# Dealing the first layer's expert groups anew over its two score loops

## The chip, the cores and the metric

The kernel runs on one core of one Trainium2 chip. The metric is the device time of one execution in microseconds, lower is better. Before the change three runs took 1210.66 to 1214.54 us, median 1212.18 us. One further execution was taken with the hardware profiler: 1208.67 us, with a span of 1206.9 us from its first to its last instruction.

## The reference

Two transformer layers on x of shape 4 x 512 x 128. Only the first layer touches the change:

```python
xn = layernorm(x)
x = x + attention0(xn) + experts0(xn)

# attention0: 16 heads, bd = 16, windows of 64 positions
strain = disp_win - disp                       # for every offset j = 0..63
bond_logits = gelu(strain @ W_strain + rel_emb @ W_pos) @ W_bond
damage      = sigmoid(gelu(strain @ W_dmg + b_dmg) @ W_dmg_out + b_dmg_out)
logits      = bond_logits - 10 * damage        # then masked softmax over the window

# experts0: 16 experts, each token goes to 4 of them
h = t @ w1.T + b1 ; s = swiglu(h) ; y = s @ w2.T + b2   # summed with the gates
```

## The kernel before, in words

The first layer is one setup block, then for each half g = 0, 1 of the heads a **score loop** and a softmax block; the second layer follows. `first_layer` builds all of it, and each block is a set of five programs, one per engine, that run side by side and meet at the block's end.

**The score loop.** A score loop has 64 items (offsets j), eight to an iteration `it` = 0..7. VectorE forms the shifted difference of an item (L757) into one of four slots of the tile `ring`, ScalarE takes the gelu (L895, or L900, L901 and L903), TensorE reduces it over the width of a head (`reduce`, L957) into the PSUM tile LG. The slot is free again when TensorE has reduced it. In five items of eight TensorE forms one of the two differences itself from the tile DS (`strain`, L981 and L985), in PSUM tile SD, instead of VectorE. DS holds three bf16 parts of the input in partitions 0 to 95 and ones in partitions 96 to 98, which add a bias. ScalarE splits the input into the parts (L935, L937), VectorE forms the remainders (L863, L870), SyncE copies them over (L669) and counts them on `d_parts`. GpSimd clears DS's margins (L730, L731) and writes the ones (L732). After each four items ScalarE takes a tanh (L911) and VectorE adds the logits (L777).

**The experts.** Tokens are sorted by expert through DRAM: in the first loop GpSimd scatters rows with 64 indirect DMAs (L741). SyncE waits for all of them before it loads the first sorted rows. 20 **groups** of four tiles of 128 tokens are then worked off between the items. A group n takes these steps:

- SyncE loads its rows (`tokens`, L649, tile xl), its first weights (`weights1`, L656, tile w1s, two groups deep) and its second weights (`weights2`, L663, tile w2s, one group deep)
- TensorE turns the rows (`turn`, L1019) and VectorE moves them to SBUF (`move_in`, L813)
- TensorE computes the hidden layer (`hidden`, L1027), VectorE and ScalarE apply the gate function (`glu_in` L821, `sig` L917, `glu_out` L828)
- TensorE computes the output (`expert_out`, L1036), VectorE moves it out (`move_out`, L835), GpSimd computes where it goes (`goals`, L712 to L718) and scatters it with four indirect DMAs (`store`, L723).

**What sets the order.** Every engine's order is written out by hand. `MOE_ITS` and `moe_groups` (L61, L103) say which iteration works on which groups: the first loop's iterations 5, 6 and 7 on groups 0 to 5, the second loop's iterations 0 to 6 on groups 6 to 19, two groups A and B to an iteration. In `body(it)` TensorE turns the next iteration's A behind `reduce(7, it)`, B behind `strain(5, it, 0)`; A's output comes after `strain(7, it, 0)`, B's output in the next iteration. SyncE's order in the second loop is: the 12 DS copies, eight first weights, four second weights, and only then the rows of the first two groups. A loop's block ends when SyncE has seen the last stores land (`d_ys`), GpSimd is done, and the other engines are through; in the second loop SyncE also starts `fetch(0)` and `fetch(1)` (L592) in it, which read the outputs back.

Of the kernel before, what the change touches and what calls it, by code (L numbers as in the profile page):

```python
# [21 lines left out]
B, T, C = 4, 512, 128  # L22
# [7 lines left out]
TP = PAD + T + 1  # L30
# [29 lines left out]
ZQ = 12  # L60
MOE_ITS = ((5, 6, 7), (0, 1, 2, 3, 4, 5, 6))  # L61
XROW = C + 2 * K0
# [40 lines left out]
def moe_groups(g, it):  # L103

    if it not in MOE_ITS[g]:
        return None, None
    first = 2 * (len(MOE_ITS[0]) * g + MOE_ITS[g].index(it))
    return first, first + 1

# [78 lines left out]
def first_layer(nc, t_in, l0, sb, psum, sem, ident, ACC, nhalf, stats, mv, rstd, carried):  # L188
# [34 lines left out]
    lones = sb("lones", [P, 4, 32], F32, l0)  # L223
# [20 lines left out]
    with ExitStack() as su:  # L244
# [332 lines left out]
    tok_turned, tok_moved, h_ready, xg_ready, sig_ready, s_ready, y_ready, y_used = (  # L577
        sem(n) for n in ("moe_turned", "moe_moved", "h_ready", "xg_ready", "sig_ready", "s_ready", "y_ready", "y_used"))
    d_scatter, d_w2, goals_ready = sem("d_scatter0"), sem("d_w2_"), sem("goals_ready")
    d_xl, d_ys, d_w1 = ([sem(f"{what}_{n}_") for n in range(2)] for what in ("d_xl", "d_ys", "d_w1"))  # L580
# [33 lines left out]
    for g in range(G):  # L614
        with ExitStack() as lp:
# [3 lines left out]
            xsT, t2 = attT[:, G - 1, 0, :], attT[:, G - 1, 1, :]  # L619
# [20 lines left out]
            PYf = PY[:].rearrange("p n c -> p (n c)")  # L640
            groups = [n for it in MOE_ITS[g] for n in moe_groups(g, it)]

            @block.sync
            def _(sp):
# [19 lines left out]

                sp.wait_ge(small_pool, 5 + 2 * g)
                for n, ready, count in ((0, parts_act, 1), (1, parts_act, 2), (2, parts_dve, 2)):
# [3 lines left out]
                if g == 0:  # L670
# [9 lines left out]
                    sp.wait_ge(small_dve, 8)  # L680
                first, end = groups[0], groups[-1] + 1
                weights1(first)
                weights1(first + 1)
                weights2(first)
                if g == 0:
                    sp.wait_ge(d_scatter, 16 * TT * K0)
                tokens(first)
                tokens(first + 1)
                for n in range(first, end, 2):
                    if n > first:  # L690
                        weights2(n)
                    if n + 2 < end:
                        weights1(n + 2)
                        tokens(n + 2)
                        weights1(n + 3)
                    weights2(n + 1)
                    if n + 2 < end:
                        tokens(n + 3)
                for n in range(2):
                    sp.wait_ge(d_ys[n], 64 * (end // 2))  # L700
                if g == G - 1:
# [4 lines left out]
            def _(pool):  # L706
# [24 lines left out]
                pool.memset(DS[0:96, :, :, PAD + T:TP], 0.0).then_inc(small_pool, 1)  # L731
                pool.memset(DS[96:99], 1.0).then_inc(small_pool, 1)  # L732
                pool.wait_ge(small_pool, 6 + 2 * g)
                for q in range(JQ - 1 if g else ZQ):
# [16 lines left out]
            def _(v):  # L751
# [85 lines left out]
                def body(it):  # L837
                    A, B_ = moe_groups(g, it)
                    before = moe_groups(g, it - 1)[1]
                    move_in(A)  # L840
# [28 lines left out]
                v.wait_ge(parts_act, 2 * g + 2)  # L869
                v.tensor_tensor(parts[2], rest, parts[1], ALU.subtract).then_inc(parts_dve, 1)  # L870
                item(1, 0)
                if g == 0:
                    tile_tables()
                item(2, 0)
                v.wait_ge(d_parts, 192 * (g + 1))
# [8 lines left out]
            def _(act):  # L884
# [29 lines left out]
                def sig(n):  # L914
                    if n is not None:
                        act.wait_ge(xg_ready, n + 1)
                        act.activation(t2[:], xg[:], ACT.Tanh, scale=ALPHA / 2).then_inc(sig_ready, 1)  # L917

                def body(it):
                    A, B_ = moe_groups(g, it)  # L920
                    gelu(2, it)
                    gelu(3, it)
                    gelu(4, it)
                    sig(A)
                    gelu(5, it)
                    tanh(0, 2 * it)
                    gelu(6, it)
                    gelu(7, it)
                    gelu(8, it)
                    gelu(9, it)  # L930
                    sig(B_)
                    tanh(1, 2 * it + 1)


                act.copy(parts[0], AD[:, 1, :, PAD:PAD + T]).then_inc(parts_act, 1)  # L935
                act.wait_ge(parts_dve, 2 * g + 1)
                act.copy(parts[1], rest).then_inc(parts_act, 1)  # L937
                gelu(0, 0)
                gelu(1, 0)
                for it in range(8):  # L940
                    body(it)

            @block.tensor
            def _(pe):
# [16 lines left out]
                def strain(n, it, half):  # L961
# [14 lines left out]
                    if n == FIRST_PE_ITEMS[0] and it == 0 and half == 0:  # L976
                        pe.wait_ge(small_pool, 6 + 2 * g)
                        pe.wait_ge(d_parts, 192 * (g + 1))
# [60 lines left out]
                def body(it):  # L1039
# [3 lines left out]
                    strain(4, it, 0)  # L1043
                    expert_out(moe_groups(g, it - 1)[1])
                    reduce(2, it)
# [20 lines left out]
                if g == 0:  # L1066
                    count()
                    starts()
                    tables()
                reduce(0, 0)  # L1070
                turn(moe_groups(g, 0)[0])
                for it in range(8):
# [1313 lines left out]
```

## Time and profile before

| What | Before |
|---|---|
| Median of three runs | 1212.18 us |
| The profiled execution: time, span | 1208.67 us, 1206.9 us |
| Mean granted TensorE clock (share of full speed) | 0.928 |
| Busy: PE, DVE, ACT, POOL | 998.7, 905.2, 781.6, 573.5 us |
| First loop's block | 40 to 331 us |
| First softmax block | 331 to 414 us |
| Second loop's block | 414 to 682 us |

PE is TensorE's matmuls, PEld its weight loads, DVE VectorE, ACT ScalarE, POOL GpSimd, SP SyncE. A small q (SPq, POOLq, PEq) means that engine's sequencer. All times in rows are in us from the span's start. A timeline row has the start, the duration, the engine and line, the operation, output and inputs, the count of merged instructions, and in brackets the engine's idle time before it with what ended it. A row on SPq lasts from its first issue to its last; the data land later. A window row has, behind its bounds and length, each engine's busy time (with the number of instructions), then the granted clock, the DMA engines' share and GB/s.

### The profile page before, as it was taken

What the parts mean: (1) busy time and instruction counts of PE and PEld (TensorE: products, weight loads), DVE (VectorE), ACT (ScalarE), POOL (GpSimd) and SP (SyncE); (2) the same over time, 40 slices, a digit from 0 to 9 for tenths busy, and PEclk for the clock granted to TensorE, in tenths of its full rate; (3) what the DMA queues carried; (4) which work ended last, traced back from release to release, by engine and by line L of the source; (5) the groups of instructions that cost most, each with busy time, mean ns of one, the idle gap of its engine ahead of it and who ended that gap; (6) DMA issues with size and microseconds to landing.
All of it is one profiled execution on the core that took longest, in us unless ns stands there. A gap on an engine that the chain in (4) does not pass through costs nothing. (4 is left out here: it accounts for less than half of the span.)

```text
span 1206.9 us, 24564 instructions
## 1 busy us (share of the span) xinstructions
PE 998.7 (83%) x9762; PEld 543.5 (45%) x9762; DVE 905.2 (75%) x1050; ACT 781.6 (65%) x840; POOL 573.5 (48%) x568
## 2 busy tenths in 40 slices
PE   6677787699569649999998687899999999999898
PEld 3422222233268514433333386753654565646533
DVE  7888788599363579999999674667768577576756
ACT  3589999599453459999999652143156666665464
POOL 5598888258555234888887510232760000000072
PEclk9779999799879869999999978999879999999999
DMA  8470100112157132222221396000132344522121
GB/s 302 122 271 32 36 31 31 45 49 67 38 161 188 24 84 59 72 73 70 70 70 33 100 254 142 24 1 1 36 105 62 105 132 124 155 84 84 47 59 45
DMA packets 117101, 105.14 MB, mean 87 GB/s; under 512 B 11551, under 2 KB 103419, under 8 KB 116347
## 3 DMA queue, kind: packets, MB, share of 16 engines
q1 hardware_dynamic: 106968, 83.24, 24.4%
q0 software_dynamic: 8448, 20.13, 5.9%
q8 instruction: 77, 1.26, 0.5%
q10 hardware_dynamic: 1571, 0.20, 0.1%
q14 instruction: 37, 0.30, 0.1%
HBM read 62.05 MB, written 38.34 MB: 83 GB/s over the span
## 5 line engine op out<-in xcount | busy, mean ns | idle before, releaser
L757 DVE SCALAR_TENSOR_TENSOR ring<-AD,PT 128x1808 f32<-128x1808 f32 (+15 forms) x128 | 282.1, 2221 | 33.2 <-PE LG L957 30.8
L957 PE MATMUL LG<-ring,lred 128*32 128x456 f32 (+15 forms) x2048 | 242.9, 595 | 17.6 <-ACT ring L895 17.6
L723 POOL DMA_INDIRECT ys<-yo,goali x80 | 168.5, 2107 | 77.8 <-DVE yo L835 54.7
L895 ACT ACTIVATE ring<-ring 128x3616 f32<-128x3616 f32 (+15 forms) x52 | 177.3, 3410 | 14.9 <-DVE ring L757 14.8
L2222 DVE TENSOR_REDUCE MX<-SS 128x2 f32<-128x1024 f32 x119 | 144.5, 1218 | 55.8 <-PE SS L1939 55.7
L2152 ACT ACTIVATE EX<-SS 128x1024 f32<-128x1024 f32 x128 | 130.4, 1031 | 78.9 <-PE SS L1939 78.4
L741 POOL DMA_INDIRECT xs<-rows,sloti x64 | 142.5, 2227 | 23.7 <-issue 19.2
L981 PE MATMUL SD<-DS,eyes 99*32 99x456 bf16 (+14 forms) x1216 | 92.0, 379 | 61.4 <-ACT ring L900 61.0
L901 ACT ACTIVATE ring<-ring 128x1824 f32<-128x1824 f32 (+14 forms) x76 | 139.0, 1829 | 0.0
L1856 POOL DMA_INDIRECT XN<-ys,sloti x16 | 16.2, 1015 | 248.0 <-PE SS L1949 243.5
L957 PEld LDWEIGHTS LG<-ring,lred 128*32 128x32 f32 x2048 | 62.0, 113 | 122.5 <-issue 93.3
L757 DVE SCALAR_TENSOR_TENSOR ring<-AD,bdmg 128x1808 f32<-128x1808 f32 (+15 forms) x52 | 114.8, 2207 | 0.0
L900 ACT ACTIVATE ring<-SD 128x912 f32<-128x912 f32 (+14 forms) x76 | 74.7, 983 | 33.6 <-PE SD L985 32.7
L981 PEld LDWEIGHTS SD<-DS,eyes 99*32 99x32 bf16 x1216 | 21.4, 96 | 158.3 <-ACT ring L900 101.2
L985 PE MATMUL SD<-DS,eyes 96*32 96x456 bf16 (+14 forms) x1216 | 90.9, 374 | 0.0
L903 ACT ACTIVATE ring<-SD 128x912 f32<-128x912 f32 (+14 forms) x76 | 74.9, 985 | 10.7 <-PE SD L985 10.6
L1939 PE MATMUL SS<-KS,QS 32*128 32x512 f32 x238 | 62.2, 516 | 14.8 <-DVE MX L2222 12.9
L1959 PE MATMUL PW<-EX,VA 128*32 128x512 f32 x512 | 69.0, 612 | 0.0
L2129 ACT ACTIVATE HB<-PHh,b1c 128x128 f32<-128x128 f32 x156 | 44.8, 371 | 37.0 <-PE PHh L1891 36.8
L1939 PE MATMUL SS<-QS,KS 32*128 32x512 f32 x256 | 65.4, 511 | 3.4 <-ACT EX L2152 2.1
L2274 DVE RECIPROCAL attT<-attT 128x128 f32<-128x128 f32 (+1 forms) x58 | 54.4, 959 | 0.2
L1212 ACT ACTIVATE zs<-wtT 128x2048 f32<-128x2048 f32 (+1 forms) x10 | 31.9, 3192 | 24.1 <-DVE wtT L1165 14.9
(407 smaller groups left out, 1739.8 us busy)
## 6 DMA issues: line engine op xcount, KB each, us to landing
w1s<-in_L_ffn_W SPq DMA_DIRECT2D x39, 256.0 KB, 3.0
w2s<-in_L_ffn_W SPq DMA_DIRECT2D x39, 256.0 KB, 2.9
band<-zs SPq DMA_DIRECT2D x8, 1024.0 KB, 10.8
wide<-band POOLq DMA_DIRECT2D x16, 380.0 KB, 8.3
wide<-band SPq DMA_DIRECT2D x16, 380.0 KB, 11.2
xl<-xs SPq DMA_DIRECT2D x20, 272.0 KB, 3.0
xs<-Z SPq DMA_DIRECT2D x5, 1024.0 KB, 8.8
w1s<-w1d SPq DMA_DIRECT2D x80, 64.0 KB, 1.8
```

What stands on the lines that cost most here:

```text
L723: pool.indirect_dma_start(ys0[:, :], bass.IndirectOffsetOnAxis(ap=goali[:, 4 * n + a:4 * n + a + 1], axis=0), yo[:, n % 2, a, :], None, bo ...
L741: pool.indirect_dma_start(xs0[:, :], bass.IndirectOffsetOnAxis(ap=sloti[:, t, k:k + 1], axis=0), rows[:, t, :], None, bounds_check=ROWS0 - ...
L757: return v.scalar_tensor_tensor(out=ring[:, slot, s, :, t0:T], in0=AD[:, s, :, j + t0:j + T], scalar=extra, in1=AD[:, s, :, PAD + t0:PAD + T],
L895: act.activation(tiles, tiles, ACT.Gelu).then_inc(gelu_done, 1)
L901: act.activation(tiles, tiles, ACT.Gelu)
L903: act.activation(ring[:, slot, 1, 2:4, t0:T], SD[:, :, t0:T], ACT.Gelu).then_inc(gelu_done, 1)
L957: mm = pe.matmul(LG[32 * b:32 * b + 32, par, s, t0:T], lred[:, s, n % 4, :], ring[:, slot, s, b, t0:T], start=(n % 4 == 0), stop=(n % 4 == 3))
L981: pe.matmul(SD[32 * q:32 * q + 32, i, t0:T], eyes[0:99, q, :], DS[0:99, q, 2 * half + i, j + t0:j + T], start=True, stop=False)
L985: mm = pe.matmul(SD[32 * q:32 * q + 32, i, t0:T], eyes[0:96, 4, :], DS[0:96, q, 2 * half + i, PAD + t0:PAD + T], start=False, stop=True)
L1939: mm = pe.matmul(bank[:, n, :], rows[r:r + 32, b % 2, q, P * t:P * t + P], cols[r:r + 32, b % 2, q, :], start=True, stop=True)
L2152: act.activation(EX[:, Q % 2, hh:hh + 2, t, :], SS[:, slot, :, :], ACT.Exp, scale=SCALE1).then_inc(freed[slot], 1)
L2222: v.tensor_reduce(MX[:, t, p // 2, hh:hh + 2], pairs_of(b, name), AX.X, ALU.max).then_inc(freed[slot], 1)
```

## The change

- **The deal.** The first loop works on groups 0 to 3 instead of 0 to 5: iteration 5 has only a B, iteration 6 two, iteration 7 only an A. The second loop works on 4 to 19: group 4 ahead of iteration 0, two groups in each of iterations 0 to 6, group 19 as A of iteration 7.
- **The group ahead.** At the second loop's head TensorE turns group 4 and computes its hidden layer before `reduce(0, 0)`, and its output behind it. ScalarE, not VectorE, moves it in and out.
- **SyncE's order.** In the second loop the rows of the first two groups and the first group's first weights are loaded before the DS copies. In both loops the later loads go group by group: `weights1(n + 2)`, `tokens(n + 2)`, `weights2(n + 1)`.
- **The ones.** GpSimd's memset of DS's rows of ones (L732) becomes four ScalarE copies, one for each quarter, between the casts and the gelus of items 0 and 1. TensorE waits for them (`ones_ready`) before its first `strain`.

```diff
-MOE_ITS = ((5, 6, 7), (0, 1, 2, 3, 4, 5, 6))
+MOE = ({5: (None, 0), 6: (1, 2), 7: (3, None)},
+       {-1: (None, 4), **{it: (5 + 2 * it, 6 + 2 * it) for it in range(7)}, 7: (19, None)})
...
-                sp.wait_ge(small_pool, 5 + 2 * g)
+                first, end = groups[0], groups[-1] + 1
+                if g:
+                    tokens(first)
+                    tokens(first + 1)
+                    weights1(first)
+                sp.wait_ge(small_pool, 5 + g)
...
-                weights1(first)
+                if g == 0:
+                    weights1(first)
                 weights1(first + 1)
                 weights2(first)
                 if g == 0:
                     sp.wait_ge(d_scatter, 16 * TT * K0)
-                tokens(first)
-                tokens(first + 1)
-                for n in range(first, end, 2):
-                    if n > first:
-                        weights2(n)
+                    tokens(first)
+                    tokens(first + 1)
+                for n in groups:
                     if n + 2 < end:
                         weights1(n + 2)
                         tokens(n + 2)
-                        weights1(n + 3)
-                    weights2(n + 1)
-                    if n + 2 < end:
-                        tokens(n + 3)
+                    if n + 1 < end:
+                        weights2(n + 1)
...
-                pool.memset(DS[96:99], 1.0).then_inc(small_pool, 1)
-                pool.wait_ge(small_pool, 6 + 2 * g)
+                pool.wait_ge(small_pool, 5 + g)
...
                 v.tensor_tensor(parts[2], rest, parts[1], ALU.subtract).then_inc(parts_dve, 1)
+                glu_in(ahead)
                 item(1, 0)
                 if g == 0:
                     tile_tables()
+                glu_out(ahead)
                 item(2, 0)
...
+                def move_in(n):
+                    if n is not None:
+                        act.wait_ge(tok_turned, n + 1)
+                        act.copy(xsT[:], PH[:]).then_inc(tok_moved, 1)
+                def move_out(n):
+                    if n is not None:
+                        act.wait_ge(y_ready, n + 1)
+                        if n >= 2:
+                            act.wait_ge(d_ys[n % 2], 64 * (n // 2))
+                        act.copy(yo[:, n % 2], PY[:]).then_inc(y_used, 1)
+                def ones_row(q):
+                    act.copy(DS[96:99, q].rearrange("p b t -> p (b t)"), lones[96:99, 0, 0:1].to_broadcast([3, B * TP])).then_inc(ones_ready, 1)
...
                 act.copy(parts[0], AD[:, 1, :, PAD:PAD + T]).then_inc(parts_act, 1)
+                move_in(ahead)
                 act.wait_ge(parts_dve, 2 * g + 1)
                 act.copy(parts[1], rest).then_inc(parts_act, 1)
+                ones_row(0)
                 gelu(0, 0)
+                sig(ahead)
+                ones_row(1)
+                ones_row(2)
                 gelu(1, 0)
+                ones_row(3)
+                move_out(ahead)
...
-                        pe.wait_ge(small_pool, 6 + 2 * g)
+                        pe.wait_ge(small_pool, 5 + g)
+                        pe.wait_ge(ones_ready, 4 * g + 4)
...
+                turn(ahead)
+                hidden(ahead)
                 reduce(0, 0)
+                expert_out(ahead)
                 turn(moe_groups(g, 0)[0])
```

## Rows read from the trace of the kernel before

**Rows 1.** Busy time by stage: us, PE, PEld, DVE, ACT, POOL, PEclk, DMA share, GB/s.

```profile
199.40:242.90 43.50, 28.16 (x308) 9.78 (x304) 28.37 (x20) 29.57 (x23) 17.68 (x22) 0.84 0.14 39
...
242.90:274.50 31.60, 28.78 (x332) 11.97 (x328) 30.47 (x28) 30.44 (x24) 19.22 (x15) 1.00 0.19 54
```

**Rows 2.** Timeline, ScalarE: the logits' tanh (start, duration, instruction, idle before it).

```profile
169.09 0.66 ACT L911 ACTIVATE Z<-LG,bdo 128x476 f32<-128x476 f32 x1
...
199.37 0.67 ACT L911 ACTIVATE Z<-LG,bdo 128x484 f32<-128x484 f32 x1
...
242.84 0.68 ACT L911 ACTIVATE Z<-LG,bdo 128x492 f32<-128x492 f32 x1
...
306.40 0.69 ACT L911 ACTIVATE Z<-LG,bdo 128x508 f32<-128x508 f32 x1
...
670.16 0.69 ACT L911 ACTIVATE Z<-LG,bdo 128x508 f32<-128x508 f32 x1
```

**Rows 3.** Timeline: the first rows of the experts arrive in the first loop.

```profile
207.75 1.81 PE L957 MATMUL LG<-ring,lred 128*32 128x488 f32 x16
...
217.54 0.94 SPq L649 DMA_DIRECT2D xl<-xs  x2
...
220.54 1.12 PE L1019 MATMUL PH<-ident,xl 128*128 128x128 f32 x4 [10.98 <-DMA xl<-xs]
...
239.14 0.66 PE L1019 MATMUL PH<-ident,xl 128*128 128x128 f32 x4
```

**Rows 4.** Timeline: end of the first loop.

```profile
310.75 0.68 DVE L835 COPY yo<-PY 128x512 f32<-128x512 f32 x1
...
322.67 0.97 POOL L723 DMA_INDIRECT ys<-yo,goali  x1 [0.30 <-issue]
...
331.14 3.51 POOL L1127 MEMSET wide<- 128x4096 f32 x1 [7.50 <-POOLq L615]
```

**Rows 5.** Timeline: end of the second loop.

```profile
668.07 1.96 POOL L723 DMA_INDIRECT ys<-yo,goali  x1 [0.30 <-issue]
...
672.71 1.79 SPq L592 DMA_DIRECT2D fetched<-ys  x1
...
680.74 0.69 DVE L777 SCALAR_TENSOR_TENSOR Z<-Z,LG 128x512 f32<-128x512 f32 x1 [9.18 <-ACT Z L911]
```

**Rows 6.** Timeline: head of the first loop.

```profile
41.24 7.77 POOL L732 MEMSET DS<- 3x9216 bf16 x1
...
41.98 5.92 PE L998 MATMUL PH<-chosen_key,attT 128*128 128x240 f32 x30
...
44.63 4.46 DVE L785 TENSOR_SCALAR attT<-attT 16x128 f32<-16x128 f32 x1
...
51.17 3.22 ACT L895 ACTIVATE ring<-ring 128x3616 f32<-128x3616 f32 x1 [3.61 <-DVE ring L757]
...
71.71 0.91 ACT L900 ACTIVATE ring<-SD 128x912 f32<-128x912 f32 x1
```

**Rows 7.** Timeline: head of the second loop.

```profile
414.04 0.94 POOL L730 MEMSET DS<- 96x1008 bf16 x1 [21.71 <-POOLq L1080]
...
416.04 9.42 SPq L669 DMA_DIRECT2D DS<-ring  x12
...
418.42 1.90 ACT L937 CAST ring<-ring 128x2048 bf16<-128x2048 f32 x1 [2.47 <-DVE ring L863]
...
420.34 1.28 ACT L895 ACT_TABLE_LOAD   x1
...
426.31 8.13 SPq L656 DMA_DIRECT2D w1s<-w1d  x8
...
441.99 1.12 PE L1019 MATMUL PH<-ident,xl 128*128 128x128 f32 x4 [13.86 <-DMA xl<-xs]
...
447.78 0.93 ACT L900 ACTIVATE ring<-SD 128x912 f32<-128x912 f32 x1 [9.80 <-PE SD L985]
```

**Rows 8.** The page's DMA issues: KB each, median us from issue to landing.

```profile
w1s<-w1d SPq DMA_DIRECT2D x80, 64.0 KB, 1.8
```

More of the change, by code:

```diff
@@ L103, in moe_groups @@
 def moe_groups(g, it):
[L105 to L108, printed above, removed]
+    return MOE[g].get(it, (None, None))
 def dram_rows(tensor, offset, dims):
@@ L578, in first_layer @@
         sem(n) for n in ("moe_turned", "moe_moved", "h_ready", "xg_ready", "sig_ready", "s_ready", "y_ready", "y_used"))
+    ones_ready = sem("ones_ready")
     d_scatter, d_w2, goals_ready = sem("d_scatter0"), sem("d_w2_"), sem("goals_ready")
@@ L640, in first_layer @@
             PYf = PY[:].rearrange("p n c -> p (n c)")
-            groups = [n for it in MOE_ITS[g] for n in moe_groups(g, it)]
+            groups = [n for it in sorted(MOE[g]) for n in MOE[g][it] if n is not None]
+            ahead = moe_groups(g, -1)[1]
             @block.sync
@@ L680, in _ @@
                     sp.wait_ge(small_dve, 8)
-                first, end = groups[0], groups[-1] + 1
-                weights1(first)
+                if g == 0:
+                    weights1(first)
                 weights1(first + 1)
@@ L694, in _ @@
                         tokens(n + 2)
-                        weights1(n + 3)
-                    weights2(n + 1)
-                    if n + 2 < end:
-                        tokens(n + 3)
+                    if n + 1 < end:
+                        weights2(n + 1)
                 for n in range(2):
-                    sp.wait_ge(d_ys[n], 64 * (end // 2))
+                    sp.wait_ge(d_ys[n], 64 * ((end + 1 - n) // 2))
                 if g == G - 1:
@@ L838, in body @@
                     A, B_ = moe_groups(g, it)
-                    before = moe_groups(g, it - 1)[1]
+                    before = moe_groups(g, it - 1)[1] if it else None
                     move_in(A)
@@ L1043, in body @@
                     strain(4, it, 0)
-                    expert_out(moe_groups(g, it - 1)[1])
+                    expert_out(moe_groups(g, it - 1)[1] if it else None)
                     reduce(2, it)
```

## The prediction

> **What bounds the kernel now.** I read the window view by stage first, to see whether an engine or a wait sets a loop's pace. In an ordinary iteration with two groups, 31.6 us long, ScalarE is busy 30.4 us and VectorE 30.5 us, and TensorE, at full clock, 28.8 us [rows 1]. The loops run at the pace of gelu and shifted difference, and the groups fit in between. The stretch from 199.4 to 242.9 is not like that: ScalarE is busy 29.6 of 43.5 us, and TensorE's mean clock is 0.84 [rows 1]. Then I read the timeline at the four places where no engine is at work: the first rows of the experts, the end of each loop, and the head of each loop. The change touches exactly these places and no other.
>
> **The first rows of the experts.** One iteration without groups takes 199.37 - 169.09 = 30.28 us, the next 242.84 - 199.37 = 43.47 us [rows 2]. TensorE is done with `reduce(7, 4)` at 209.56 and then stands for 10.98 us in front of `turn(0)`, whose rows SyncE may load only when the scatter is through, at 217.54, and which land 3.0 us later [rows 3]. After that TensorE starts at the low clock: four transposes take 1.12 us there and 0.66 us at 239.14 [rows 3]. In the new deal the first turn is that of B in iteration 5. The two turns of that iteration stand 239.14 - 220.54 = 18.6 us apart [rows 3], so TensorE comes to it at about 209.6 + 18 = 227, 6 us after the rows landed today. The stall goes altogether. Slices widen from 484 to 492 columns, so the iteration would take 30.28 x 492 / 484 = 30.8 us: **-12.7 us**. Bounds: -11.0, the stall alone, and -13.2, no widening. Next late is nothing: the loop is back at ScalarE's pace. Two groups fewer in iterations 5 to 7 give little, since iterations 5 and 6 with groups take (306.40 - 242.84) / 2 = 31.8 us against some 31.3 us by the same widening: **-0.3 us** for the lighter halves.
>
> **End of the first loop.** The last store ends 7.50 us before the next block starts, at 323.64, and GpSimd's sequencer is what ends that wait [rows 4]; VectorE and ScalarE have been idle since about 318. So the block ends by the last store plus 7.5 us. With group 3 as A of iteration 7 the last moving-out is that of 310.75, ending at 311.43 [rows 4]; without B's hidden layer and gate in front of it I put it 1.3 us earlier (at least the 0.66 us that four products of this size take, at most 2), at 310.1. Four stores of 0.97 us with 0.30 us between them [rows 4] are 4.8 us, and 0.9 us pass before the first (an estimate): last store done at 315.8, block over at 323.3. **-7.8 us**. Bounds: if the 7.5 us is really 4.5 us, as the nearest bound at the second loop's end allows, -10.8; if nothing of the gate's time comes free, -6.
>
> **End of the second loop.** Here today's last group is out in time: the last store ends at 670.03, SyncE has issued both fetches by 674.50, and VectorE ends last, at 681.43 [rows 5]. Now group 19 is A of iteration 7. One tanh more on ScalarE and its company cost 0.4 us, and the moving-out ends 3.7 us behind the tanh (310.1 - 306.40, [rows 2]), at 670.16 + 0.4 + 3.7 = 674.3. The last store ends 5.7 us later, at 680.0. From there SyncE needs what it needs today, 674.50 - 670.03 = 4.5 us [rows 5], so the block ends at 684.5 instead of 681.7: +2.8 us. With GpSimd's 7.5 us as in the first loop it is +5.8. I take the middle, **+4 us**: the same engine's wait applies, but here it is not seen. What the fetches read is used only after four softmax steps, some 20 us later, which hides their 10 us delay.
>
> **Head of the first loop.** GpSimd's memset of the ones lasts to 49.01, and VectorE's `tensor_scalar` on 16 x 128 elements, issued at 44.63, ends at 49.09: 4.46 us for a tiny operation, let go by the memset [rows 6]. ScalarE's first gelu then starts at 51.17, after 3.61 us of waiting [rows 6]. Without the memset VectorE is 4.3 us earlier, but its `token_slots` needs TensorE's counts, which end at 47.90 [rows 6]; so the differences of items 1 to 3 come only about 2.1 us earlier. ScalarE pays four ones: 2304 elements each, by the cast of 2048 in 1.90 us [rows 7] 2.1 us, 8.5 us in all. The first copy takes the time in which ScalarE loads its table today, and the table load, 1.28 us [rows 7], moves behind it. By my walk: casts done at 46.3, ones 48.4, load 49.7, gelu to 52.9, two ones to 57.2, gelu from 58.1 (VectorE) to 61.3, ones to 63.4, two gelus to 69.8. The first gelu from SD starts at 71.71 today [rows 6]: **-1.9 us**. Bounds: -4.3, all that the held operation lost, and +2, if a copy on three partitions costs a quarter more. In the second loop nothing waits for the memset.
>
> For a change of table the Trainium skill (ScalarE: Activation LUTs, What ACT_TABLE_LOAD costs) gives 2.66 us with the drain. Rows 7 show 1.28 us from 420.34, begun 0.02 us behind the cast. By the page the sum would be 1.4 us less gain in each loop, 2.8 us in all; I go by the row.
>
> **Head of the second loop.** The block starts at 414.04, and SyncE's queue delays everything: DS copies from 416.04 to 425.46, first weights to 434.44, second weights behind them, rows last; TensorE stands 13.86 us for them, ScalarE 9.80 us, until 447.78 [rows 7]. Now the rows go first and land at about 417.1 (3.0 us [rows 3]). ScalarE: cast, `move_in` at 418.4 (0.6 us), second cast to 420.9 (0.5 later than today's 420.32), ones, table load, gelu from 424.3 to 427.5, tanh to 428.2, two ones to 432.4, gelu to 435.6, ones to 437.7. SyncE: 1.0 us for the rows, four first weights at 8.13 / 8 + 0.1 = 1.1 us each [rows 7] to 419.4, twelve DS copies of 0.65 us to 427.2 (1.7 later than today, still before VectorE's item 3 needs the slot), four and four weights to 436, landed 1.8 us later [rows 8]: 437.4. So `expert_out(4)` runs to 438.6, at the low clock; `move_out` to 439.2; two gelus of 3.2 us to 445.7, by which time TensorE has turned 5, reduced item 1 and formed item 4. Start of the SD gelu at 445.7 instead of 447.78: **-2.1 us**, with group 4 done. Bounds: -3.5, if nothing waits for the second weights, and +2, if landings take 4 us beside the DS copies. Queued behind `expert_out(4)` on TensorE is `reduce(1)`, so any delay of the second weights is one of the loop.
>
> **Sum.** -12.7 - 0.3 - 7.8 + 4 - 1.9 - 2.1 = -20.8 us. The profiled execution would take 1208.67 - 20.8 = 1187.9 us. It lies 3.5 us under the median of the runs; against that median the forecast is **1191.4 us**. Differences within 0.3%, 3.6 us, are about what a measurement of this kernel cannot tell from none.
>
> **Rivals.**
> - **The ends dominate.** If GpSimd's 7.5 us holds at both ends and the ones cost more than they free (heads at +1 together), the gain is 12.7 + 0.3 + 7.8 - 5.8 - 1 = 14 us: 1198. For it: the wait of 7.50 us is in the trace once. Against it: it is seen once only. Chance 0.2.
> - **More than the sum.** If the wait behind the last store is 4.5 us at both ends, the ends give -10.8 + 2.8 and the sum is -25 us: 1187. Chance 0.22.
> - **The stall moves, it does not go.** If the scatter lasted until 227 in the first loop, B's turn would wait as A's does. It is GpSimd's own queue and nothing in it grows, and it starts earlier. The gain would be some 8 us: 1204. Chance 0.04.
> - **The lock turns round.** Group 4's and 5's `goals` on GpSimd now fall among VectorE's differences at the head. By the Trainium skill (SBUF — State Buffer, SBUF: two separate sides) a VectorE operation with two SBUF inputs and a GpSimd operation that reads SBUF exclude each other, and whoever starts first keeps the port. By rows the memset held a one-input operation for 4.3 us [rows 6]; fourteen small operations are not longer than that together, so +3 us at most: 1194. It lies within my range and has 0.06.
> - **Slower: the low clock.** TensorE now begins the second loop in short pieces between SyncE's landings, and after today's stall in the first it ran at 1.2 GHz at first (1.12 against 0.66 us [rows 3]). At that level an iteration's 28.8 us of TensorE become 28.8 x 1.12 / 0.66 = 49 us, 17 us over ScalarE's pace. From one and a quarter such iterations at the head of the second loop the whole gain is gone; two make 1191.4 + 34.6 = 1226. Against it: after the stall of 11 us the clock is back within one iteration (0.84 over that stretch, 1.00 in the next [rows 1]). Chance 0.03.
>
> My own case has 0.45. **Numbers.** The range leaves out the low clock, the moved stall and the tails: 1184 to 1199. Faster 0.95, within 0.3% 0.02, slower 0.03.
>
> **What would show it.** Right: no wait of TensorE on xl in the first loop, and 30.8 us between its fourth and fifth pair of tanhs; the first softmax block some 23 us earlier; `tensor_scalar` at the first head under 0.3 us; ScalarE's ones at 2.1 us each; the second loop from its block's start to the first SD gelu 31.7 us instead of 33.7; the second softmax block starting 4 us later relative to the last tanh. Wrong: ones of 3 us or more, a second table load in a head, TensorE standing on w2s in front of every output, or GpSimd still busy when the loops' last difference is long reduced, by more than 6 us.

## The result and the profile after

On one chip the changed kernel takes 1190.67 us in the median of four runs (1189.83 to 1192.84), the kernel before 1213.36 us (four runs, 1210.66 to 1216.69): a ratio of 0.9847, 95% interval 0.9817 to 0.9877. The forecast was 1191.4 us, range 1184 to 1199. The two profiled executions lie 18.8 us apart, 1206.9 and 1188.1 us of span.

The stall comes first again. ScalarE's tanhs in the timeline of the changed kernel answer to [rows 2]:

```profile
166.77 0.66 ACT L913 ACTIVATE Z<-LG,bdo 128x476 f32<-128x476 f32 x1
...
197.04 0.67 ACT L913 ACTIVATE Z<-LG,bdo 128x484 f32<-128x484 f32 x1
...
227.77 0.67 ACT L913 ACTIVATE Z<-LG,bdo 128x492 f32<-128x492 f32 x1
...
291.32 0.69 ACT L913 ACTIVATE Z<-LG,bdo 128x508 f32<-128x508 f32 x1
...
644.74 0.69 ACT L913 ACTIVATE Z<-LG,bdo 128x508 f32<-128x508 f32 x1
```

From 197.04 to 227.77 pass 30.73 us where 43.47 passed before. The window view of that stretch and the turn of the first rows (timeline, TensorE) show why; they answer to [rows 1, 3]:

```profile
197.04:227.77 30.73, 23.72 (x296) 7.62 (x292) 26.25 (x14) 28.91 (x21) 20.93 (x20) 1.00 0.11 33
```

```profile
212.35 0.94 SPq L649 DMA_DIRECT2D xl<-xs  x2
...
224.07 0.66 PE L1044 MATMUL PH<-ident,xl 128*128 128x128 f32 x4
```

TensorE comes to the rows 11.7 us after they were issued, with no wait in brackets, and its granted clock is 1.00 over the stretch (the window row's third number from the end), the higher of its two levels.

The end of the first loop and of the second, timeline of the changed kernel, to be held against [rows 4, 5]:

```profile
293.68 0.69 DVE L835 COPY yo<-PY 128x512 f32<-128x512 f32 x1 [1.62 <-PE PY L1061]
...
299.03 0.97 POOL L724 DMA_INDIRECT ys<-yo,goali  x1 [0.30 <-issue]
...
306.84 3.51 POOL L1155 MEMSET wide<- 128x4096 f32 x1 [6.84 <-POOLq L614]
...
647.09 0.69 DVE L835 COPY yo<-PY 128x512 f32<-128x512 f32 x1 [1.61 <-PE PY L1061]
...
652.75 0.97 POOL L724 DMA_INDIRECT ys<-yo,goali  x1 [0.30 <-issue]
...
655.32 0.69 DVE L777 SCALAR_TENSOR_TENSOR Z<-Z,LG 128x512 f32<-128x512 f32 x1 [6.95 <-ACT Z L913]
...
656.39 1.94 SPq L591 DMA_DIRECT2D fetched<-ys  x1
...
659.24 3.51 POOL L1155 MEMSET wide<- 128x4096 f32 x1 [5.52 <-POOLq L614]
```

Both blocks now end by the last store plus a wait of GpSimd's sequencer: 6.84 us in the first loop, 5.52 us in the second, where VectorE, which was last before, is done 3.2 us earlier and SyncE's last issue 0.9 us earlier. The first softmax block starts at 306.84 instead of 331.14, 24.3 us earlier; some 23 were forecast.

The two heads, same view, against [rows 6, 7]:

```profile
45.43 0.28 DVE L785 TENSOR_SCALAR attT<-attT 16x128 f32<-16x128 f32 x1
...
47.09 2.11 ACT L934 CAST DS<-lones 3x2304 bf16<-3x2304 f32 x1
49.21 1.28 ACT L897 ACT_TABLE_LOAD   x1
...
69.56 0.91 ACT L902 ACTIVATE ring<-SD 128x912 f32<-128x912 f32 x1
...
388.96 0.93 SPq L649 DMA_DIRECT2D xl<-xs  x2
390.69 3.72 SPq L656 DMA_DIRECT2D w1s<-w1d  x4
394.52 7.84 SPq L674 DMA_DIRECT2D DS<-ring  x12
403.17 3.73 SPq L656 DMA_DIRECT2D w1s<-w1d  x4
408.04 3.65 SPq L663 DMA_DIRECT2D w2s<-w2d  x4
...
413.25 2.05 PE L1061 MATMUL PY<-w2s,xg 128*128 128x128 f32 x8 [7.11 <-issue]
...
415.33 0.59 ACT L931 COPY yo<-PY 128x512 f32<-128x512 f32 x1 [2.54 <-PE PY L1061]
...
422.18 0.92 ACT L902 ACTIVATE ring<-SD 128x912 f32<-128x912 f32 x1
```

The `tensor_scalar` that was held for 4.46 us takes 0.28. In the second head the queue of SyncE is as forecast, but the second weights are its last part, TensorE's output products need 2.05 us at the low clock, and ScalarE stands 2.54 us in front of `move_out`, with two gelus of 3.2 us behind it.

A table of stages, worked out from such timeline rows of each kernel, serves for all that follows. Head 1 and 2: from ScalarE's first cast in a loop to its first gelu from SD. Iteration 4: between the second tanhs of iterations 3 and 4. Tail 1 and 2: from the loop's last tanh to the softmax block. Steady: iterations 1 to 6 of the second loop. Soft 1, 2 and last: blocks whose code the change doesn't touch; another such block of 17.7 us, between soft 2 and last, is left out. The runs behind the first pair were made on three chips, A, B and C. Each row of the table is one profiled execution.

| Kernel, chip | head 1 | it. 4 | tail 1 | soft 1 | head 2 | steady | tail 2 | soft 2 | last |
|---|---|---|---|---|---|---|---|---|---|
| before, first | 31.7 | 41.3 | 14.9 | 82.9 | 33.7 | 184.2 | 1.7 | 94.4 | 413.1 |
| changed, first | 28.8 | 30.5 | 5.7 | 82.1 | 33.3 | 184.2 | 4.6 | 95.3 | 415.8 |
| changed, B | 29.9 | 30.5 | 5.7 | 79.2 | 33.1 | 184.2 | 4.6 | 97.7 | 413.9 |
| five ahead, B | 28.9 | 30.5 | 14.6 | 83.4 | 33.3 | 184.2 | 1.7 | 95.6 | 421.1 |
| w2 first, B | 28.7 | 30.5 | 5.7 | 79.9 | 30.6 | 184.2 | 4.6 | 97.4 | 410.4 |
| both, B | 29.5 | 30.5 | 5.7 | 79.3 | 27.4 | 184.2 | 4.3 | 98.4 | 416.1 |
| ones GpSimd, A | 31.7 | 30.5 | 5.7 | 81.4 | 33.1 | 189.2 | 4.3 | 98.7 | 462.6 |
| old deal, A | 29.7 | 42.6 | 13.9 | 83.3 | 28.7 | 189.3 | 1.7 | 95.6 | 462.2 |
| ones alone, A | 28.8 | 30.8 | 14.6 | 81.7 | 35.0 | 184.2 | 1.7 | 95.0 | 462.9 |
| out later, A | 28.7 | 30.5 | 5.7 | 80.8 | 32.4 | 189.3 | 4.5 | 96.2 | 465.5 |
| before, C | 31.7 | 41.2 | 13.9 | 83.2 | 34.2 | 184.4 | 1.7 | 95.1 | 465.8 |
| ones alone, C | 29.4 | 41.5 | 14.6 | 82.8 | 34.1 | 184.4 | 1.7 | 95.1 | 462.4 |
| five first, C | 28.7 | 30.5 | 14.3 | 83.7 | 28.7 | 189.1 | 4.2 | 97.8 | 463.7 |
| store early, C | 29.9 | 30.5 | 2.7 | 78.9 | 33.2 | 189.2 | 1.7 | 96.1 | 461.6 |

Chips A and C are slower in the last block, at a mean granted clock of 0.88 to 0.89 instead of 0.93 to 0.96, so kernels are compared by their ratios to the kernel before on the same chip, and by stages.

### The profile page after: what moved, and what is told of

It reads as the page before. It is cut to its first block and busy times, and to the rows that moved or that the text cites. A ratio compares the mean times of both kernels' runs of the same rounds, so it can differ in the third digit from the quotient of the medians.

```text
span 1188.1 us, 24570 instructions
## 1 busy us (share of the span) xinstructions
PE 997.7 (84%) x9762; PEld 545.6 (46%) x9762; DVE 900.7 (76%) x1048; ACT 798.7 (67%) x850; POOL 567.9 (48%) x566
## 5 line engine op out<-in xcount | busy, mean ns | idle before, releaser
L981 PE MATMUL LG<-ring,lred 128*32 128x456 f32 (+15 forms) x2048 | 237.4, 583 | 11.0 <-ACT ring L897 11.0
L2180 ACT ACTIVATE EX<-SS 128x1024 f32<-128x1024 f32 x128 | 130.3, 1031 | 80.3 <-PE SS L1967 78.9
L741 POOL DMA_INDIRECT xs<-rows,sloti x64 | 139.0, 2173 | 28.5 <-issue 19.2
L1903 PEld LDWEIGHTS PW<-w2s,HB 128*128 128x128 f32 x312 | 40.5, 201 | 19.2 <-issue 10.9
```

The source lines that it names most:

```text
L741: pool.indirect_dma_start(xs0[:, :], bass.IndirectOffsetOnAxis(ap=sloti[:, t, k:k + 1], axis=0), rows[:, t, :], None, bounds_check=ROWS0 - ...
L981: mm = pe.matmul(LG[32 * b:32 * b + 32, par, s, t0:T], lred[:, s, n % 4, :], ring[:, slot, s, b, t0:T], start=(n % 4 == 0), stop=(n % 4 == 3))
L2180: act.activation(EX[:, Q % 2, hh:hh + 2, t, :], SS[:, slot, :, :], ACT.Exp, scale=SCALE1).then_inc(freed[slot], 1)
```

## The experiments

**The ones alone.** The old deal, with SyncE's order at the second head as before; the ones are ScalarE's. The later loads still go group by group, as in the changed kernel, so this is not quite the kernel before with one edit.

```diff
-MOE = ({5: (None, 0), 6: (1, 2), 7: (3, None)},
-       {-1: (None, 4), **{it: (5 + 2 * it, 6 + 2 * it) for it in range(7)}, 7: (19, None)})
+MOE = ({5: (0, 1), 6: (2, 3), 7: (4, 5)},
+       {it: (6 + 2 * it, 7 + 2 * it) for it in range(7)})
...
-                if g:
-                    tokens(first)
-                    tokens(first + 1)
-                    weights1(first)
```

> Groups and the order of SyncE's loads as before; only the ones are written by ScalarE. Mine: first head 3 us shorter, second head 33.7 us as before since TensorE waits for the rows at the end of SyncE's queue: 1213.4 - 3 = 1210.4 us. Rival (four copies, 8.4 us, lie on ScalarE's path in the second loop): 1215 us or more. Rival (no effect of the memset): 1213.4 us.

1260.24 us, ratio 1.0017 (0.9984 to 1.0051). Head 1 is 2.9 us shorter, head 2 no shorter (35.0): as I expected by stages, though the median shows none of it. What I had not expected is iteration 4: in this execution the stall is absent (30.8 us) with the deal of before. It is also the fastest of this kernel's twelve runs, 1251.45 us, 8.8 us under their median, so the median need not show what the profile shows.

**The stall, drawn again.** Two kernels once more, one execution each, on chip C:

> The kernel before as it is, for a second draw of the stall. Mine: the scatter's 64 transfers end somewhere between 151 and 163 us after they began at 54.5; iteration 4 to 5 takes 30.5 us plus what the rows (scatter's end + 4.4 us) are later than 209.6, plus some 1 us for the low clock: between 30.5 and 43. Rival (the stall is the same in each execution): 41 us.

> The kernel in which only the ones go to ScalarE, for another draw. Mine: the scatter begins 2 us earlier than in the kernel before; if it lasts over 158 us the stall is there (iteration of some 40 us), if it ends by 205 it is not, as in its first profile (30.8 us). Rival (moving the ones takes the stall away as such): no stall here either, whatever the scatter lasts.

1265.12 and 1258.01 us, with the stall in both: 43.6 and 43.4 us from the first tanh of iteration 4 to that of iteration 5. With 161.0 us of scatter the ones alone have the stall, with 151.4 us they had not; the rival, that moving the ones takes it away, is out. The loads of the rows and the first turn, timelines of the ones alone on A, on C, and of the kernel before on C:

```profile
205.02 0.94 SPq L649 DMA_DIRECT2D xl<-xs  x2
...
211.95 0.66 PE L1039 MATMUL PH<-ident,xl 128*128 128x128 f32 x4
```

```profile
214.38 0.94 SPq L649 DMA_DIRECT2D xl<-xs  x2
...
217.25 1.11 PE L1039 MATMUL PH<-ident,xl 128*128 128x128 f32 x4 [9.58 <-DMA xl<-xs]
```

```profile
217.20 0.94 SPq L649 DMA_DIRECT2D xl<-xs  x2
...
220.10 1.12 PE L1019 MATMUL PH<-ident,xl 128*128 128x128 f32 x4 [10.89 <-DMA xl<-xs]
```

The same kernel has the stall or not, by when the 64 transfers of the scatter are through. Over all fourteen profiles they last between 151.4 and 163.1 us for the same code; the rows were issued between 205.0 and 219.3. So -12.7 us is what this pair drew. Of the five profiles with the old deal one has next to no stall (31.1 us between those tanhs), the others 43.4 to 44.4 us. None of the nine with the new deal has it. The least slack among them is in the one whose rows were issued last, at 219.34: landed by my estimate at 222.3 (3.0 us, [rows 3]), with TensorE's turn at 225.71, 3.4 us later.

**The old deal with the new order of loads.** The diff is the first half of the one above, the deal alone.

> The groups are dealt as before (two in each of iterations 5 to 7, then two in each of 0 to 6); the ones stay with ScalarE, and the second loop's head loads rows and first weights first. Mine: the stall of 12.7 us in the first loop comes back, its end costs 9.2 us more and the second loop's end 3 us less, the second head has no group in it and no wait for the second weights, so it takes some 26 us instead of 33.3: 1190.7 + 12.7 + 9.2 - 3.0 - 7 = 1202.6 us, 11 us under the kernel before. Rival (the second head is set by the DS copies and items 1 to 3, whatever is loaded first): 33 us as before, 1209.6 us.

1262.17 us, ratio 1.0009 (0.9982 to 1.0036). By stages my theory holds in the main: iteration 4 42.6, tail 1 13.9, tail 2 1.7, and head 2 28.7 us, not the 26 that I had expected, nor the rival's 33. Against the ones alone (35.0 and 34.1) the order of loads alone is worth 5.4 to 6.3 us at the second head, and against the changed kernel the group ahead costs 4.6. That the median shows nothing has its place in the table: the steady iterations take 189.3 us instead of 184.2 (see the last section), which takes back most of what the heads gave.

**The ones back on GpSimd.**

```diff
+                pool.memset(DS[96:99], 1.0).then_inc(ones_ready, 1)
...
-                ones_row(0)
```

> The ones of the three extra rows go back to one GpSimd memset in each loop; all else as changed. Mine: at the first head VectorE's tensor_scalar is held again for 4.5 us and the first gelu from SD comes 3 us later (28.8 us becomes some 31.7); at the second head the 8.4 us of copies were in the wait for the second weights anyway, so it stays at 33.3 us; together 1193.7 us. Rival (the copies are the limit at the second head): the second head gains 6 us or more, first head loses 3, so 1188 us or less. Rival (the memset cost nothing, the table load moved something else): 1190.7 us and no difference at the first head.

1248.71 us, ratio 0.9914 (0.9883 to 0.9946). Head 1 is back at 31.7, head 2 stays (33.1). Timeline, head of the first loop:

```profile
41.68 7.77 POOL L733 MEMSET DS<- 3x9216 bf16 x1
...
45.07 4.46 DVE L787 TENSOR_SCALAR attT<-attT 16x128 f32<-16x128 f32 x1
```

The hold is there again to the hundredth. The median does not fit so well: no changed kernel ran on this chip, but the next one, with the ones on ScalarE and the output moved out later, has 1239.70 us, 9.0 us less, of which the profiles show 3.0 at the first head and 0.7 at the second. The rest is open.

**Moving the output out later.**

```diff
                     gelu(2, it)
+                    if it == 0:
+                        move_out(ahead)
...
-                move_out(ahead)
```

> As changed, but ScalarE moves the output of the group at a loop's head out behind the gelu of item 2 instead of ahead of it. Mine: ScalarE's idle 2.54 us in front of that copy at the second head go, the first gelu from SD comes 2.5 us earlier after the block's start (33.3 becomes 30.8): 1188.2 us. Rival (what item 4 waits for on TensorE, behind the output products, is late by itself): no gain, 1190.7 us; TensorE's wait moves to the SD gelu.

1239.70 us, ratio 0.9836 (0.9798 to 0.9875). The first gelu from SD comes 0.9 us earlier, not 2.5: my expectation was wrong, its rival nearly right. By the end of iteration 0 nothing is left of it (54.9 us from the loop's start to the second tanh, 54.8 in the changed kernel). ScalarE's wait moved one step on (timeline, ScalarE):

```profile
421.76 0.93 ACT L902 ACTIVATE ring<-SD 128x912 f32<-128x912 f32 x1 [1.75 <-PE SD L1011]
```

TensorE, which waits for the second weights before its next turn and the products of SD, is the limit.

**The second weights first.** The edit above, and in the second loop `weights2(first)` ahead of `weights1(first + 1)`.

> As changed, but at the second loop's head SyncE loads the second weights of the first group before the first weights of the second, and ScalarE moves that group's output out behind the gelu of item 2. Mine: the second weights land at 19.6 us after the block's start instead of 24.4, TensorE's output products, the next turn and item 4 follow 4 us earlier, ScalarE has no wait, and the first gelu from SD comes at 30.4 instead of 33.3: 3 us under the changed kernel. Rival (the first weights of the second group, 5 us later now, hold hidden in front of item 4): the first gelu from SD at 32.5 us as with the copy alone moved, 1 us or less.

1183.92 us, ratio 0.9764 (0.9723 to 0.9804), beside 1189.82 us and 0.9815 (0.9786 to 0.9843) for the changed kernel on the same chip:

> The changed kernel as it is, to have its stages and its ratio on the same chip as the others of this call. Mine: ratio to the kernel before 0.98 to 0.985; first gelu from SD 28.8 us after the first loop's start and 33.3 us after the second's. Rival (the last stage, which no edit touches, differs between the two kernels by more than 2 us in the same direction as in the first pair of profiles): then part of the change's result lies there.

The second weights are issued at 400.01 instead of 403.83, 14.4 instead of 19.1 us after the start of the block, and the gelu comes 2.5 us earlier (30.6). At the end of iteration 0 only 0.9 us of it is left (53.8 against 54.7 us from the loop's start to the second tanh). TensorE, once more at the low clock (sixteen products of `reduce` take 1.73 us from 412.86 and 2.91 us from 418.06, and the granted clock is 0.68 in the mean from 418.0 to 423.3), holds ScalarE at item 5 (timeline):

```profile
422.32 0.93 ACT L905 ACTIVATE ring<-SD 128x912 f32<-128x912 f32 x1 [2.15 <-PE SD L1014]
```

So of the 5.9 us between the two medians the stages of the loop show 0.9. In the profiles 3.5 us more lie in the last block, which no edit touches; how much of the medians' difference belongs to the edit is not shown.

**Both, and the ones of the second loop on GpSimd.** The edits of the kernel before this one, and besides:

```diff
+                if g:
+                    pool.memset(DS[96:99], 1.0).then_inc(ones_ready, 1)
...
                 def ones_row(q):
+                    if g:
+                        return
```

> As the kernel with the second weights first and the output moved out later, and besides the ones of the second loop are written by one GpSimd memset; those of the first loop stay with ScalarE. Mine: at the second head 8.4 us of copies go from ScalarE, and now that it no longer waits for the second weights this counts: first gelu from SD at some 27 us after the block's start, limited by the landing of the next group's first weights; 6 us under the changed kernel in all. Rival (VectorE's differences are the limit at the head): no more than the 3 us of the kernel without this edit.

1183.17 us (1172.67 to 1187.77), ratio 0.9751 (0.9708 to 0.9793): 6.6 us under the changed kernel on the same chip, though the intervals touch. Head 2 takes 27.4 us, and to the end of iteration 0 it is 49.1 us, against 54.7 in the changed kernel and 53.8 with the second weights first: of the 8.4 us of copies 4.7 count as soon as the weights no longer cover them. The median doesn't show them: it lies 0.8 us under that of the kernel with the second weights first, and in the profiles the last block is 5.7 us longer here.

**Five groups in the first loop, one ahead.**

```diff
+MOE = ({5: (None, 0), 6: (1, 2), 7: (3, 4)},
+       {-1: (None, 5), **{it: (6 + 2 * it, 7 + 2 * it) for it in range(7)}})
```

> Groups dealt so: first loop none in the first half of iteration 5, then five groups up to the second half of iteration 7; one ahead of the second loop, two in each of its iterations 0 to 6, none in the last. Mine: only the two ends differ from the changed kernel: the first loop's end is back at some 14 us after its last tanh (+9), the second's at 1.7 instead of 4.6 (-3): 6 us over the changed kernel. Rival (what the second end gave back was the low clock in the softmax behind it): its softmax block also gains, so 5 us or less over.

1198.54 us, ratio 0.9873 (0.9831 to 0.9914), 8.7 over the changed kernel. Tail 1 is 8.9 us longer, tail 2 2.9 shorter, both as expected. The first softmax block is 4.2 us longer (83.4 against 79.2), which I had not expected, and the second 2.1 shorter, as the rival had it, though not its total of 5 us or less. The profiles differ by more than the medians, since the last block is 7.2 us longer in this one.

**Five in the first loop, none ahead.** As above, with groups 5 to 18 in iterations 0 to 6 and `7: (19, None)`.

> Groups dealt so: five in the first loop as in the kernel with five and one ahead; nothing ahead of the second loop; two in each of its iterations 0 to 6 and group 19 in the first half of iteration 7. Mine: against the changed kernel the first loop's end is 9 us longer (14.6 after its last tanh), the second head shorter by 4.6 (first gelu from SD at 28.7 us, as with the old deal and the new order of loads), the second end equal (4.6): 4.4 us over the changed kernel, some 1194.5 on a chip that gives it 1190. Rival (the group ahead costs nothing at the head, and the old deal's shorter head came from elsewhere): first gelu from SD at 33 us, 9 us over.

1254.79 us, ratio 0.9929 (0.9886 to 0.9971). Head 2 is 28.7 as expected, tail 1 14.3, tail 2 4.2. Against the profiles with the new deal the group ahead costs 4.4 to 4.6 us at its head, for 8.6 us at the tail of the first loop.

**The last stores early.** The rows of groups 3 and 19 get the output of groups 2 and 18.

```diff
-                    pool.wait_ge(y_used, n + 1)
+                    early = n in (3, 19)
+                    pool.wait_ge(y_used, n + 1 - early)
...
+                sp.wait_ge(y_used, end)
```

> As changed, but GpSimd stores the last group of each loop as soon as it has stored the one before, from that one's buffer (so the rows of groups 3 and 19 get another group's output); VectorE still forms and moves out the right output, and SyncE waits for that before it fetches. Mine: what ends both loops is the last store plus GpSimd's 5.5 to 7.5 us behind it; with the store out of the way both softmax blocks start 1.7 us after the last tanh, as the second did before: 4.0 us less at the first end, 2.9 at the second, 7 us in all. Rival (the blocks wait for the moving-out, not for stores and GpSimd): under 1 us at each end.

1233.94 us, ratio 0.9787 (0.9760 to 0.9814). The second softmax block starts 1.7 us after the last tanh, as expected. In the first loop I was 1.0 us off (2.7), and the reason is in GpSimd's timeline:

```profile
295.84 0.97 POOL L726 DMA_INDIRECT ys<-yo,goali  x1 [0.30 <-issue]
303.65 3.51 POOL L1157 MEMSET wide<- 128x4096 f32 x1 [6.84 <-POOLq L614]
```

The wait behind the last store is the same 6.84 us, so it sets the block's start even here.

## Why the prediction was right, and where its terms were off

The two large terms, the stall and the end of the first loop, came by the mechanisms named. The median's nearness to the forecast (0.7 us) is in part luck: the terms below add up to -21.9 us, their errors going both ways, and blocks that the change doesn't touch add 3.6.

**The stall** (-12.7): measured 43.47 - 30.73 = 12.7 us in this pair, by the mechanism named. What the forecast lacked is that it is a draw. The rival of the moved stall was set too far off: it asked for a scatter until 227, but TensorE came at 224.07, and the rows land 4.3 us behind the scatter's end (216.20 and 220.50 in the kernel before), so 219.8 would have been enough. The latest end seen is 218.00, in the kernel with the ones on GpSimd, whose scatter starts 2.7 us later.

**Lighter halves** (-0.3): nothing; iterations 5 and 6 take (291.32 - 227.77) / 2 = 31.8 us each, as before. In this pair two groups fewer change nothing there.

**End of the first loop** (-7.8, bounds -10.8 and -6): -9.2. The stores end 8.7 us after the tanh instead of the 9.4 I walked, and the wait behind them is 6.84 instead of 7.50. I had taken the 7.50 for a constant. Over the runs it is 6.84 with 4 groups stored in the first loop, 7.17 with 5 (both kernels with five) and 7.50 with 6.

**End of the second loop** (+4, the middle of 2.8 and 5.8): +3.0, and 0.3 more in the last iteration. The middle was taken between two mechanisms, and the measured value lies near the 2.8 of the wrong one: SyncE's last issue ends 4.6 us behind the last store, as forecast, but the block goes on until GpSimd's wait of 5.52 us is over. It is the mechanism of the 5.8, with a shorter wait. The softmax block behind it is longer too: 95.3 us in the mean of the seven profiles with a tail of 1.7, 97.4 in the seven with 4.2 to 4.6. In this pair that is 0.9 us. One place of it is TensorE's first sixteen transposes, timelines of the changed kernel and of five ahead on chip B:

```profile
654.96 3.65 PE L1290 MATMUL ZT<-ident,Z 128*128 128x128 f32 x16 [4.74 <-PEq L614]
```

```profile
666.57 1.94 PE L1290 MATMUL ZT<-ident,Z 128*128 128x128 f32 x16 [1.81 <-PEq L614]
```

The first stand behind 4.74 us of idleness and run at a granted clock of 0.50, the second behind 1.81 us and at 1.00.

**Head of the first loop** (-1.9): -2.9. The walk was right to 0.1 us up to the third of the ones; then the second gelu, which I had wait 0.9 us for VectorE, did not wait. VectorE goes by TensorE's counts, whose last products I held fixed at 5.92 us; they took 5.12. Their end is a draw too, 6.7 to 8.2 us after the loop's start over the profiles. The eleven heads with the ones on ScalarE go by it: 28.7 to 28.9 us with counts done by 7.2 us, 29.4 to 29.9 with counts at 7.7 and later, while the three with the memset all take 31.7. With the counts of the kernel before, at 7.9, the forecast of -1.9 is about what comes out. The ones cost 2.11 us each, as forecast.

**Head of the second loop** (-2.1): -0.4, the worst term. The step that failed is "`expert_out(4)` runs to 438.6": I had it end 24.6 us after the block's start, and it ends 26.4 us after it. Half of the 1.8 us is SyncE's: TensorE starts on the weights 24.4 us after the start instead of 23.4. Of that 0.4 us is a slip of the sum (436 and 1.8 is 437.8, not 437.4). Besides, the rows take 1.7 us of the queue instead of 1.0 and the DS copies with the pause behind them 8.7 instead of 7.8, of which the weights (0.93 us for each issue, not 1.1) and the landing give back 1.1. The other half is the clock: the products take 2.05 us at the low clock, for which the forecast had 1.2. Eight of the same size take 1.06 from 431.96, at the high one. What lay behind, a copy and two gelus, I had right. In the kernel with the second weights first the output products begin 4.6 us and the gelu 2.5 us earlier, where moving the copy alone gave 0.9: the head hung on these weights.

For the table load I had gone by the row, 1.28 us, against the 2.66 us that the Trainium skill (ScalarE: Activation LUTs, What ACT_TABLE_LOAD costs) gives with its drain. The changed kernel decides for the row: copy to 49.20, load from 49.21, gelu from 50.51, in a place where no load stood before.

**Untouched blocks.** The first loop starts 0.8 us later, the first softmax block is 0.8 us shorter, the last block 2.7 us longer. Over the profiles of one chip the last block varies from 410.4 to 421.1 us for the same code. Its length goes with the granted clock there: 410.4 us at 0.958, 413.9 at 0.951, 416.1 at 0.943, 421.1 at 0.931, and in the first pair 413.1 at 0.950 and 415.8 at 0.943. So most of what separates the profiles (-18.8) from the sum of the measured terms (-21.9) lies in blocks that nobody changed; between the medians it is -22.7, where -20.8 were forecast.

**Rivals.** "The ends dominate" and "more than the sum" both hung on whether the wait of GpSimd is 7.5 or 4.5; it lies between. Low clock: TensorE does begin the second loop at the low clock, but the window from 443.74 to 529.00 has 1.00; it costs single places, as the output products above, no iterations. Reversed lock: no held operation of VectorE was seen in the heads of the changed kernel; it is GpSimd's small ones that are held. In the second head the same operation takes 0.22 us while VectorE stands idle, and 2.17 us beside one of VectorE's differences of 2.09 us (timeline, GpSimd):

```profile
395.48 0.22 POOL L715 TENSOR_TENSOR match<-match,xl 128x16 f32<-128x16 f32 x1
...
399.38 2.17 POOL L715 TENSOR_TENSOR match<-match,xl 128x16 f32<-128x16 f32 x1
```

**Signs.** Named beforehand as signs of being right, and seen: no wait on xl in the first loop, 30.7 us between the tanhs, the earlier softmax block, `tensor_scalar` at 0.28 us, the ones at 2.11 us. Not seen: 31.7 us in the second head, which took 33.3. Of the signs of being wrong, TensorE stood on w2s once, in that head, and not in front of every output.

## What to carry to other kernels

When a load is wanted just after a long chain of indirect transfers, put its first use behind the latest end that several profiles show, not behind that of a single one. What is gained differs from one execution to the next, as the stall does. Put no step behind the last-issued weights at a head, where a queue is deep and the clock low; what an engine copies in such a wait is free only until the wait is gone. And at a block's end look at the last indirect transfer first: here the engine's own wait of 5.3 to 7.5 us came on top.

## What the runs showed of the hardware

- The wait of GpSimd's sequencer between the last indirect transfer and the next block follows the number issued in the block: 80 transfers (64 of the scatter, 16 stores) 6.84 us, 84 7.17, 88 7.50, and 64 in the second loop 5.52. That is 0.083 us for each and 0.2 us besides; with 60 in the second loop it would be 5.2, measured 5.30. That it is the number as such, and not what goes with it, was not tried by itself.
- ScalarE's table load took 1.28 us in each of its four places in the changed kernel. In the two heads it began 0.02 us after the end of a copy, and the gelu 0.01 us after the load's end.
- The same 64 indirect transfers took 151.4 to 163.1 us from one execution to the next.
- The first softmax block takes 83.0 us in the mean of the seven profiles with a tail of 13.9 us and more in front of it, 80.2 in the seven with 5.7 us and less. No run isolates why.
- On chips A and C five kernels take 189 us for the six steady iterations, three others on the same chips 184.2 to 184.4, as all on B do. The five load the rows first at the second head, the three don't; but on B the same order costs nothing. And iterations 5 and 6 of the first loop take 64.9 to 65.1 us in all eight profiles on A and C, whatever the order of loads, against 63.6 in the six others; so the chip seems to have a part in it. In the waits of the kernel with the early store, over iterations 1 to 3 (total, times, longest), one row is new against the changed kernel on B:

```profile
ACT ring L907 <- PE SD L1012: 3.6, 3, 1.3
```

By the records the products of that SD half had ended 1.2 us before ScalarE went on. The cause stays open. The 5 us account for most of why the old deal with the better head was no faster than the kernel before.
